# Two rounds of expert selection moved from the routing stage into the end of the first layer's attention

## The chip, the cores and the metric

The kernel runs on one core of a Trainium2 chip. Its engines work in parallel, each through its own instruction stream, and meet only at semaphores: TensorE (PE, with weight loads shown apart as PEld), VectorE (DVE), ScalarE (ACT), GpSimd (POOL) and SyncE (SP, which here only issues DMAs). The metric is the device time of one execution in microseconds, median of several; lower is better.

## The reference

Input x is 16 sequences of 256 tokens of 128 numbers, so 4096 tokens or 32 tiles of 128. Two layers follow, each x + s * g of the layer-normalised x.

- Layer 0: s is a gated linear recurrence (causal convolution, two sigmoid gates, scan, output matrix, RMS norm). g is the silu of a transformer block: layer norm, 16-head attention with heads of 8, output projection, residual, layer norm, then a mixture of 8 experts of which each token takes 2.
- Layer 1: s is attention with normalised queries and keys, g is a gated feed-forward net whose operands are rounded to blockwise FP4.

What the change touches is the choice of the two experts:

```
h = layernorm(x + attention)            # 4096 tokens x 128
logits = h @ gate_w + gate_b            # 4096 x 8
topv, topi = top_k(logits, 2)           # ties go to the lower expert
gw = softmax(topv)
ew = sum(one_hot(topi) * gw)            # weight of every expert for every token
moe = einsum(expert outputs, ew)
```

## The kernel before

The program is a row of phases: `phase_pre0` (norms, queries, keys, values), `phase_attention(0)`, `phase_moe`, `phase_update`, `phase_attention(1)`, `phase_ffn1`. Between two phases every engine meets at a barrier: each finishes its own instructions, POOL clears semaphores in between, and only then does any engine start on the next phase. Within a phase the order of each engine's work is written out by hand; there is no scheduler.

**Attention.** It goes sequence by sequence (b = 0 to 15), 16 steps each. PE computes scores and products, ACT the exponentials, and DVE takes the largest score of each query beforehand (`take_maximum`, L387, `neg_max`). The output of sequence b is divided, transposed and projected (`norm`, L1076 to L1087) during the next sequence, b+1. DVE then computes mean and variance (`statistics`, `variances`, ending in `ve`, L1107), and POOL's `rows_ready(c)` (L1017 to L1027) turns them into the normalised rows `hn` and the logits of the two tiles of sequence c, and increments `hn_ready`. SP stores `hn` to DRAM (L952) once `hn_ready` says so. The phase ends in a tail. In the last sequence DVE has no maxima left to take (they are always for the next sequence). After it come the three norm stages of sequence 15, its statistics, POOL's `rows_ready(15)`, and SP's last store, whose landing SP waits for before it goes to the barrier.

**Routing,** the start of `phase_moe`. DVE alone starts. It sets `one8` and `more_b` (the second is the multiplier of a scan that starts afresh at each expert), and then runs `best(0)` and `best(1)`: the largest logit of each token (`top`), which experts have it (`key`), times a falling order so that the lowest expert wins (`key`, `kmax`), and a one-hot mask (`mask`). Between the two the chosen logit is pushed far down. These are 11 instructions over 128 x 256 (32 tiles x 8 experts), each waiting for the one before (`link`). `sel` is the sum of both masks in another order, `upto` a running count; PE sums them over partitions, and DVE goes on to a place for every token, to slots, and to index lists. POOL's gathers and SP's weight loads wait for these lists. From there 72 slots of 128 tokens go through the experts.

The instructions of one step are waited for by a semaphore counter: `Steps.link` marks an instruction and waits for its mark before the next one.

Of the kernel before, what the change touches and what calls it, by code (L numbers as in the profile page):

```python
# [27 lines left out]
P = 128  # L28
# [8 lines left out]
E = 8  # L37
# [87 lines left out]
class Shared:  # L125
# [10 lines left out]
    def sem(self, name):  # L136
        return self.nc.alloc_semaphore(self.name(name))
# [18 lines left out]
def build(nc, x, vecs, b1v, mats, w1, w2, b2, gate_w, rows, gate_b, w4, consts, more, out):  # L156
    with ExitStack() as top:
# [55 lines left out]
        with ExitStack() as layer0:  # L213
# [14 lines left out]
            S.w2_sb = S.sb(experts, "w2", [P, E, FC, D])  # L228

# [587 lines left out]
def phase_attention(S, layer):  # L817
# [9 lines left out]
    with ExitStack() as ctx:  # L827
# [26 lines left out]
        if layer == 0:  # L854
# [5 lines left out]
            stats_done, mv_done, var_ready, rstd_ready, hn_ready, lg_scaled = (  # L860
                sem(n) for n in ("stats_done", "mv_done", "var_ready", "rstd_ready", "hn_ready", "lg_scaled"))
# [189 lines left out]
        def _(dve):  # L1051
# [79 lines left out]

            dve.sem_inc(bank_free, N_BANK)  # L1132
            if layer == 0:
                dve.sem_inc(hn_ready, 2)
            dve.memset(p_o[:], 0.0).then_inc(o_set, 1)
            sequences(dve, seq)
            for stage in range(len(NORM)):
                i = len(LAST) + stage
                consume(NB - 1, 1, base(NB - 1, "last") + i, bank_of("last", NB - 1, i), ("norm", stage))
            if layer == 0:  # L1140
                statistics(NB - 1, 1, base(NB - 1, "last") + len(LAST) + len(NORM) + N_BANK)
                variances(NB - 1, 1)

# [138 lines left out]
def phase_moe(S):  # L1282
# [4 lines left out]
    with ExitStack() as ctx:  # L1287
# [3 lines left out]
        key = sb("key", [P, N, E])  # L1291
        mask = [sb(f"mask{k}", [P, N, E]) for k in range(2)]
        top = [sb(f"top{k}", [P, N]) for k in range(2)]
        kmax = [sb(f"kmax{k}", [P, N]) for k in range(2)]
        gap, ex, den = sb("gap", [P, N]), sb("ex", [P, N]), sb("den", [P, N])
        sel, upto = sb("sel", [P, E, N], BF16), sb("upto", [P, E, N], BF16)
        more_b = sb("more_b", [P, E, N])
# [145 lines left out]
        def _(dve):  # L1443
            st = Steps(dve, steps)
            lg = S.logits

            def best(k):

                st.link(dve.tensor_reduce(top[k][:], lg[:], AX.X, ALU.max))
                st.link(dve.tensor_tensor(key[:], lg[:], of_tile(top[k]), ALU.is_equal))  # L1450
                st.link(dve.tensor_tensor(key[:], key[:], of_expert(const("order", E)), ALU.mult))
                st.link(dve.tensor_reduce(kmax[k][:], key[:], AX.X, ALU.max))
                st.link(dve.tensor_tensor(mask[k][:], key[:], of_tile(kmax[k]), ALU.is_equal))

            st.mark(dve.memset(one8[:], 1.0))
            st.link(dve.memset(more_b[:], 1.0))
            st.mark(dve.memset(more_b[:, :, 0:1], 0.0))
            best(0)
            st.link(dve.scalar_tensor_tensor(lg[:], mask[0][:], -3.0e38, lg[:], ALU.mult, ALU.add))
            best(1)  # L1460
# [1046 lines left out]
```

## Time and profile before

| | us |
|---|---|
| median of 3 runs | 1036.28 (1034.65 to 1038.63) |
| profiled execution, its own time | 1034.11 |
| its span, first to last instruction | 1032.3 |
| DVE busy | 806.2 (78%) |
| PE busy | 804.6 (78%) |
| ACT busy | 612.8 (59%) |
| POOL busy | 397.3 (38%) |
| mean granted TensorE clock | 0.881 of full speed |

The shares are averages over very different stages, and no engine is at its limit throughout. The stage that the change touches is short: the attention of layer 0 lies between about 80.9 and 293.9 us, and routing between 293.9 and about 325 us. What matters there is who waits for whom in those few microseconds, which the trace shows instruction by instruction. In its rows PEclk is the clock granted to TensorE, where 1.00 is 2.4 GHz and 0.50 is 1.2 GHz.

### The profile page before, as it was taken

What the parts mean: (1) busy time and instruction counts of PE and PEld (TensorE: products, weight loads), DVE (VectorE), ACT (ScalarE), POOL (GpSimd) and SP (SyncE); (2) the same over time, 40 slices, a digit from 0 to 9 for tenths busy, and PEclk for the clock granted to TensorE, in tenths of its full rate; (3) what the DMA queues carried; (4) which work ended last, traced back from release to release, by engine and by line L of the source; (5) the groups of instructions that cost most, each with busy time, mean ns of one, the idle gap of its engine ahead of it and who ended that gap; (6) DMA issues with size and microseconds to landing.
All of it is one profiled execution on the core that took longest, in us unless ns stands there. A gap on an engine that the chain in (4) does not pass through costs nothing. (4 is left out here: it accounts for less than half of the span.)

```text
span 1032.3 us, 23120 instructions
## 1 busy us (share of the span) xinstructions
PE 804.6 (78%) x6866; PEld 472.2 (46%) x6866; DVE 806.2 (78%) x1738; ACT 612.8 (59%) x1270; POOL 397.3 (38%) x684
## 2 busy tenths in 40 slices
PE   4888899999806788888896455649999999776764
PEld 3643333333305677776775233313333333345553
DVE  6758899999666345565663899889999998799984
ACT  3866677777705366566653478747777777433342
POOL 6852343333413666676673132231111211022332
PEclk9977999999955899999998666659999999888987
DMA  4692422222102343343342145532222221000001
GB/s 138 230 305 65 140 78 84 73 74 78 32 6 59 115 145 119 122 124 123 122 129 95 61 142 169 175 126 66 69 76 64 75 66 33 1 1 21 13 19 30
DMA packets 114716, 94.52 MB, mean 92 GB/s; under 512 B 10783, under 2 KB 102714, under 8 KB 114512
## 3 DMA queue, kind: packets, MB, share of 16 engines
q1 hardware_dynamic: 109104, 83.31, 25.9%
q0 software_dynamic: 4608, 8.93, 2.9%
q10 hardware_dynamic: 928, 1.32, 0.4%
q8 instruction: 41, 0.67, 0.3%
q14 instruction: 35, 0.29, 0.1%
HBM read 59.18 MB, written 34.08 MB: 90 GB/s over the span
## 5 line engine op out<-in xcount | busy, mean ns | idle before, releaser
L1157 ACT ACTIVATE pr<-score 128x512 f32<-128x512 f32 x512 | 279.1, 599 | 109.7 <-PE score L1225 109.6
L387 DVE TENSOR_REDUCE neg_max<-bank 128x2 f32<-128x512 f32 x480 | 303.7, 683 | 7.5 <-PE bank L371 6.3
L1225 PE MATMUL score<-qs,ks 51*128 51x256 bf16 x1024 | 179.3, 277 | 13.5 <-DVEq L1132 5.6
L371 PE MATMUL bank<-ks,qs 48*128 48x256 bf16 x960 | 168.4, 278 | 0.0
L1243 PE MATMUL p_o<-pr,vs 128*18 128x256 f32 x2048 | 164.2, 391 | 0.6 <-ACT pr L1157 0.6
L1225 PEld LDWEIGHTS score<-qs,ks 51*128 51x128 bf16 x1024 | 64.8, 95 | 155.7 <-DVE neg_max L387 49.3
L396 POOL TENSOR_TENSOR max_parts<-neg_max,one 128x16 bf16<-128x16 f32 x64 | 14.3, 223 | 268.6 <-DVE neg_max L387 259.9
L1428 POOL DMA_INDIRECT y_scratch<-y_all,to_i x72 | 79.9, 1109 | 56.0 <-DVE y_all L1529 45.1
L1644 ACT ACTIVATE hid<-p_ha,b_slot 128x128 f32<-128x128 f32 x144 | 44.9, 364 | 89.8 <-PE p_hd L1755 63.3
L1422 POOL DMA_INDIRECT y_all<-hn_scratch,token_i x72 | 76.1, 1056 | 55.6 <-DVEq L1510 34.0
L1529 DVE COPY y_all<-p_y 128x128 f32<-128x128 f32 x72 | 20.9, 290 | 83.3 <-PE p_y L1766 40.5
L1766 PE MATMUL p_y<-w,hid 128*128 x576 | 85.5, 293 | 0.0
L1766 PEld LDWEIGHTS p_y<-w,hid 128*128 128x128 f32 x576 | 71.5, 195 | 5.2
L1521 DVE TENSOR_SCALAR hid<-p_hd,b_slot 128x128 f32<-128x128 f32 x144 | 43.4, 343 | 24.8 <-PE p_hd L1755 19.6
L371 PEld LDWEIGHTS bank<-ks,qs 48*128 48x128 bf16 x960 | 60.5, 95 | 2.3
L285 POOL TENSOR_TENSOR hq<-hn,amax_h 128x1408 f32<-128x1408 f32 x7 | 18.1, 2589 | 102.6 <-DVE hn L263 102.6
L1243 PEld LDWEIGHTS p_o<-pr,vs 128*18 128x18 f32 x2048 | 36.2, 96 | 44.0 <-issue 30.8
L2413 PE MATMUL p_z<-wd_t,hq_t 128*128 128x128 f32 (+1 forms) x192 | 31.8, 340 | 22.4 <-ACT hq_t L2343 22.4
L1755 PE MATMUL p_ha<-h_t,w_now 128*128 128x128 f32 x288 | 46.2, 285 | 0.0
L1755 PE MATMUL p_hd<-h_t,w_now 128*128 128x128 f32 x288 | 46.0, 284 | 0.0
L2134 PE MATMUL p_qkv<-mat,xn_t 128*128 128x384 f32 x64 | 37.6, 757 | 7.4 <-ACT xn_t L2069 7.4
L2413 PEld LDWEIGHTS p_z<-wd_t,hq_t 128*128 128x128 f32 (+1 forms) x192 | 30.1, 249 | 24.7 <-ACT hq_t L2343 24.7
(324 smaller groups left out, 1645.0 us busy)
## 6 DMA issues: line engine op xcount, KB each, us to landing
w_now<-w_dram SPq DMA_DIRECT2D x72, 256.0 KB
ks<-k_scratch SPq DMA_DIRECT2D x128, 96.0 KB, 2.2
qs<-q_scratch SPq DMA_DIRECT2D x128, 96.0 KB, 2.3
k_scratch<-parts SPq DMA_DIRECT2D x16, 384.0 KB, 2.7
q_scratch<-parts SPq DMA_DIRECT2D x16, 384.0 KB, 3.0
k_scratch<-parts SPq DMA_DIRECT2D x16, 256.0 KB, 2.3
q_scratch<-parts SPq DMA_DIRECT2D x16, 256.0 KB, 2.6
both<-y_scratch SPq DMA_DIRECT2D x8, 512.0 KB, 4.0
```

The costliest lines, as they stand in the source:

```text
L371: return pe.matmul(bk[:, qt * L:(qt + 1) * L], S.qs[u][rows, place(h), qt * P:(qt + 1) * P], S.ks[u][rows, place(h), :], start=True, stop= ...
L387: return dve.tensor_reduce(S.neg_max[:, h // (H // 2), :, col:col + 1], bk[:].rearrange("p (q t) -> p q t", t=L), AX.X, ALU.max, negate=True)
L1157: act.activation(pr[s % N_PR][:, 2 * k:2 * k + 2, :], score[k][:], ACT.Exp, scale=SCALE).then_inc(exp_done, 1)
L1225: scored = pe.matmul(score[k][:, j, :], ks[u][rows, place(h), kt * P:(kt + 1) * P], qs[u][rows, place(h), :], start=True, stop=True)
L1243: last = pe.matmul(p_o[32 * j:32 * j + 2 * VW, hg // 2, 0:L], vs[u][:, kt, hg * JT + j, :], pr[s % N_PR][:, j, :], start=s % (STEPS // 2) ...
L1422: pool.indirect_dma_start(blk[j % U], None, S.hn_scr, bass.IndirectOffsetOnAxis(ap=token_i[:, j:j + 1], axis=0), bounds_check=last_token, ...
L1428: pool.indirect_dma_start(S.y_scr, bass.IndirectOffsetOnAxis(ap=to_i[:, j:j + 1], axis=0), y_out[j % U], None, bounds_check=last_row, oob_ ...
L1521: last = dve.tensor_scalar(hid[r][:, f, :], part(r, f), b1_slot[:, f, j:j + 1], 0.0, ALU.add, ALU.max)
L1644: last = act.activation(hid[r][:, f, :], part(r, f), ACT.Relu, bias=b1_slot[:, f, j:j + 1])
L1755: last = pe.matmul(part(r, f), w1_now[j % 3][:, f * P:(f + 1) * P], h2_t[r][:], start=True, stop=True)
L1766: last = pe.matmul(p_y[j % 2][:, 0:D], hid[j % 2][:, f, :], S.w2_sb[:, bass.ds(e, 1), f, :].rearrange("p o c -> p (o c)"), start=False, st ...
L2413: last = pe.matmul(p_z[:, n * D:(n + 1) * D], hq_t[0:w, i, n * P:(n + 1) * P], S.wd_t[0:w, i, :], start=i == 0, stop=i == len(K_CHUNKS) - 1)
```

## The change

A new function `best_two(first, end)` holds both rounds, for the tiles first to end. DVE runs it twice inside `phase_attention(0)`: over tiles 0 to 27 right after the last sequence's own work and before the norm stages of sequence 15, and over tiles 28 to 31 after the variances of sequence 15. Each call first waits for POOL's `hn_ready`: for the logits of sequence 13, or of sequence 15. The masks, `top` and `more_b` are allocated in the scope that spans both phases. The two memsets of `more_b`, with a wait between them, go to the start of DVE's attention work, in front of the memset of `p_o`. The routing stage begins with `sel`, and `one8` is set behind the scan.

```diff
--- before.py
+++ after.py
@@ -226,6 +226,9 @@
             S.both = [S.sb(layer0, f"both{u}", [P, NT, 2, D]) for u in range(2)]
             experts = layer0.enter_context(ExitStack())
             S.w2_sb = S.sb(experts, "w2", [P, E, FC, D])
+            S.mask = [S.sb(experts, f"mask{k}", [P, S.NTILE, E]) for k in range(2)]
+            S.top = [S.sb(experts, f"top{k}", [P, S.NTILE]) for k in range(2)]
+            S.more_b = S.sb(experts, "more_b", [P, E, S.NTILE])
 
 
             with nc.cleanup_on_exit():
@@ -857,8 +860,10 @@
                              for n, shape in (("mv", [2, 2]), ("ve", [2]), ("x_now", [2, ROW])))
             hn = [sb(f"hn{u}", [P, 2, D]) for u in range(2)]
             lg_raw = sb("lg_raw", [P, 2, E])
-            stats_done, mv_done, var_ready, rstd_ready, hn_ready, lg_scaled = (
-                sem(n) for n in ("stats_done", "mv_done", "var_ready", "rstd_ready", "hn_ready", "lg_scaled"))
+            key, kmax = sb("key", [P, S.NTILE, E]), [sb(f"kmax{k}", [P, S.NTILE]) for k in range(2)]
+            stats_done, mv_done, var_ready, rstd_ready, hn_ready, lg_scaled, steps_top, more_set = (
+                sem(n) for n in ("stats_done", "mv_done", "var_ready", "rstd_ready", "hn_ready", "lg_scaled", "steps_top",
+                                 "more_set"))
             hn_kept = [sem("hn_kept0"), sem("hn_kept1")]
         else:
             NX = GROUP // BLK
@@ -1129,17 +1134,41 @@
                     if layer == 1 and kind == "last" and s == 4:
                         first_input()
 
+            def best_two(first, end):
+
+                dve.wait_ge(hn_ready, end // 2 + 2)
+                now = slice(first, end)
+                shape = [P, end - first, E]
+                lg, keys = S.logits[:, now, :], key[:, now, :]
+                order = S.more[:, MORE["order"]:MORE["order"] + E].unsqueeze(1).broadcast_to(shape)
+                of_tile = lambda t: t[:, now].unsqueeze(2).broadcast_to(shape)
+                for k in range(2):
+                    if k:
+                        to.link(dve.scalar_tensor_tensor(lg, S.mask[0][:, now, :], -3.0e38, lg, ALU.mult, ALU.add))
+                    to.link(dve.tensor_reduce(S.top[k][:, now], lg, AX.X, ALU.max))
+                    to.link(dve.tensor_tensor(keys, lg, of_tile(S.top[k]), ALU.is_equal))
+                    to.link(dve.tensor_tensor(keys, keys, order, ALU.mult))
+                    to.link(dve.tensor_reduce(kmax[k][:, now], keys, AX.X, ALU.max))
+                    to.link(dve.tensor_tensor(S.mask[k][:, now, :], keys, of_tile(kmax[k]), ALU.is_equal))
+
             dve.sem_inc(bank_free, N_BANK)
             if layer == 0:
+                to = Steps(dve, steps_top)
                 dve.sem_inc(hn_ready, 2)
+                dve.memset(S.more_b[:], 1.0).then_inc(more_set, 1)
+                dve.wait_ge(more_set, 1)
+                dve.memset(S.more_b[:, :, 0:1], 0.0)
             dve.memset(p_o[:], 0.0).then_inc(o_set, 1)
             sequences(dve, seq)
+            if layer == 0:
+                best_two(0, 2 * (NB - 2))
             for stage in range(len(NORM)):
                 i = len(LAST) + stage
                 consume(NB - 1, 1, base(NB - 1, "last") + i, bank_of("last", NB - 1, i), ("norm", stage))
             if layer == 0:
                 statistics(NB - 1, 1, base(NB - 1, "last") + len(LAST) + len(NORM) + N_BANK)
                 variances(NB - 1, 1)
+                best_two(2 * (NB - 2), 2 * NB)
 
         @block.scalar
         def _(act):
@@ -1288,13 +1317,9 @@
         sb = lambda n, shape, dt=F32: S.sb(ctx, n, shape, dt)
         sem = S.sem
 
-        key = sb("key", [P, N, E])
-        mask = [sb(f"mask{k}", [P, N, E]) for k in range(2)]
-        top = [sb(f"top{k}", [P, N]) for k in range(2)]
-        kmax = [sb(f"kmax{k}", [P, N]) for k in range(2)]
+        mask, top, more_b = S.mask, S.top, S.more_b
         gap, ex, den = sb("gap", [P, N]), sb("ex", [P, N]), sb("den", [P, N])
         sel, upto = sb("sel", [P, E, N], BF16), sb("upto", [P, E, N], BF16)
-        more_b = sb("more_b", [P, E, N])
         above = sb("above", [P, N, E])
         nb, ends, start, one8 = sb("nb", [P, E]), sb("ends", [P, E]), sb("start", [P, E]), sb("one8", [P, E])
         place, picked = sb("place", [P, N, E]), [sb(f"picked{k}", [P, N, E]) for k in range(2)]
@@ -1442,26 +1467,11 @@
         @block.vector
         def _(dve):
             st = Steps(dve, steps)
-            lg = S.logits
-
-            def best(k):
-
-                st.link(dve.tensor_reduce(top[k][:], lg[:], AX.X, ALU.max))
-                st.link(dve.tensor_tensor(key[:], lg[:], of_tile(top[k]), ALU.is_equal))
-                st.link(dve.tensor_tensor(key[:], key[:], of_expert(const("order", E)), ALU.mult))
-                st.link(dve.tensor_reduce(kmax[k][:], key[:], AX.X, ALU.max))
-                st.link(dve.tensor_tensor(mask[k][:], key[:], of_tile(kmax[k]), ALU.is_equal))
-
-            st.mark(dve.memset(one8[:], 1.0))
-            st.link(dve.memset(more_b[:], 1.0))
-            st.mark(dve.memset(more_b[:, :, 0:1], 0.0))
-            best(0)
-            st.link(dve.scalar_tensor_tensor(lg[:], mask[0][:], -3.0e38, lg[:], ALU.mult, ALU.add))
-            best(1)
             by_expert = lambda t: t[:].rearrange("p n e -> p e n")
             st.link(dve.tensor_tensor(sel[:], by_expert(mask[0]), by_expert(mask[1]), ALU.add))
             flat = lambda t: t[:].rearrange("p e n -> p (e n)")
             dve.tensor_tensor_scan(flat(upto), flat(more_b), flat(sel), 0.0, ALU.mult, ALU.add).then_inc(sel_ready, 1)
+            st.mark(dve.memset(one8[:], 1.0))
             dve.tensor_tensor(gap[:], top[1][:], top[0][:], ALU.subtract).then_inc(gap_ready, 1)
 
             dve.wait_ge(counted, 1)
```

On DVE, around the end of the attention and the start of routing, this stood in a row before (the two branches are the phase boundary; `o_rec` to `ve_193` are the norm stages and statistics of sequence 15):

```order
L1107 TENSOR_SCALAR ve_192<-mv_190 128x2
L1076 RECIPROCAL o_rec<-bank_168 128x32
...
L1107 TENSOR_SCALAR ve_193<-mv_191 128x2
L827 UNCONDITIONAL_BRANCH
L1442 UNCONDITIONAL_BRANCH
L1455 MEMSET one_224 128x8
L1456 MEMSET more_b 128x256
L1457 MEMSET more_b 128x8
L1449 TENSOR_REDUCE top_210<-logits 128x32
L1450 TENSOR_TENSOR key<-logits,top_210 128x256
...
L1453 TENSOR_TENSOR mask_209<-key,kmax_213 128x256
L1462 TENSOR_TENSOR sel<-mask_208,mask_209 128x256
```

The same place of the changed kernel:

```order
L1112 TENSOR_SCALAR ve_197<-mv_195 128x2
L1148 TENSOR_REDUCE top_84<-logits 128x28
L1149 TENSOR_TENSOR key<-logits,top_84 128x224
...
L1152 TENSOR_TENSOR mask_83<-key,kmax_206 128x224
L1081 RECIPROCAL o_rec<-bank_173 128x32
...
L1112 TENSOR_SCALAR ve_198<-mv_196 128x2
L1148 TENSOR_REDUCE top_84<-logits 128x4
L1149 TENSOR_TENSOR key<-logits,top_84 128x32
...
L1152 TENSOR_TENSOR mask_83<-key,kmax_206 128x32
L830 UNCONDITIONAL_BRANCH
L1467 UNCONDITIONAL_BRANCH
L1471 TENSOR_TENSOR sel<-mask_82,mask_83 128x256
```

The 11 selection instructions over 256 columns are now 11 over 224 ahead of `o_rec`, and 11 over 32 between `ve` and the boundary.

On DVE at the start of the attention, before:

```order
L461 UNCONDITIONAL_BRANCH
L1050 UNCONDITIONAL_BRANCH
L1135 MEMSET p_o 128x1024
L387 TENSOR_REDUCE neg_max<-bank_168 128x2
```

and in the changed kernel:

```order
L464 UNCONDITIONAL_BRANCH
L1055 UNCONDITIONAL_BRANCH
L1158 MEMSET more_b 128x256
L1160 MEMSET more_b 128x8
L1161 MEMSET p_o 128x1024
L390 TENSOR_REDUCE neg_max<-bank_173 128x2
```

Two memsets now stand ahead of `p_o` and of the first maximum. On PE, ACT, POOL and SP no instruction moves.

## Rows read from the trace of the kernel before

**Rows 1.** Who waited for whom, 274 to 325 us: total, times, longest.

```profile
DVE one L1455 <- PEq L233: 6.1, 1, 6.1
PE p_y L1724 <- DVE upto L1464: 14.6, 1, 14.6
```

**Rows 2.** Stretches: length; busy (count) PE, PEld, DVE, ACT, POOL; PEclk; DMA; GB/s.

```profile
80.90:87.80 6.90, 6.45 (x54) 2.29 (x58) 5.44 (x9) 3.81 (x8) 2.77 (x9) 0.50 0.01 4
...
278.60:283.30 4.70, 3.72 (x36) 1.19 (x36) 0.02 (x1) 3.08 (x7) 3.00 (x6) 1.00 0.10 31
...
293.90:299.30 5.40, 0.00 (x0) 0.00 (x0) 4.96 (x14) 0.00 (x0) 0.00 (x0) 0.50 0.01 2
...
345.00:350.00 5.00, 5.00 (x20) 3.69 (x18) 1.10 (x4) 0.98 (x3) 2.42 (x3) 0.50 0.22 81
355.00:360.00 5.00, 4.37 (x36) 3.82 (x35) 2.31 (x7) 3.80 (x10) 3.11 (x3) 1.00 0.45 153
```

**Rows 3.** DVE in time, routing: start, us, line, operation, [idle before <- releaser].

```profile
293.89 0.07 DVE L1455 MEMSET one<- 128x8 f32 x1 [6.08 <-PEq L233]
293.97 0.27 DVE L1456 MEMSET more_b<- 128x256 f32 x1
294.29 0.41 DVE L1449 TENSOR_REDUCE top<-logits 128x32 f32<-128x256 f32 x1
...
299.31 0.62 DVE L1462 TENSOR_TENSOR sel<-mask,mask 128x256 bf16<-128x256 f32 x1
...
301.38 0.42 DVE L1468 TENSOR_TENSOR above<-p_y,more 128x256 f32<-128x256 f32 x1 [0.65 <-PE p_r L1726]
```

**Rows 4.** DVE in time, end of the last sequence.

```profile
278.45 0.17 DVE L1107 TENSOR_SCALAR ve<-mv 128x2 f32<-128x2 f32 x1
283.39 0.36 DVE L1076 RECIPROCAL o_rec<-bank 128x32 f32<-128x32 f32 x1 [4.77 <-PE bank L1193]
```

**Rows 5.** POOL in time, rows and logits of sequences 13, 14 and 15.

```profile
274.67 0.22 POOL L1027 TENSOR_TENSOR logits<-lg_raw,gshift 128x16 f32<-128x16 f32 x1
278.77 0.72 POOL L1017 TENSOR_TENSOR rstd<-ve,m_half 128x2 f32<-128x2 f32 x1 [3.88 <-DVE ve L1107]
...
281.55 0.22 POOL L1027 TENSOR_TENSOR logits<-lg_raw,gshift 128x16 f32<-128x16 f32 x1
...
290.73 0.22 POOL L1027 TENSOR_TENSOR logits<-lg_raw,gshift 128x16 f32<-128x16 f32 x1
```

**Rows 6.** SP's last store of hn in time, and landing times of all of them.

```profile
290.97 0.37 SPq L952 DMA_DIRECT2D hn_scratch<-hn  x1
...
DMA to landing us min/median/max: 1.8/1.9/4.9
```

**Rows 7.** DVE in time, linked short instructions in routing.

```profile
302.69 0.17 DVE L1472 TENSOR_TENSOR start<-ends,nb 128x8 f32<-128x8 f32 x1
302.89 0.42 DVE L1473 SCALAR_TENSOR_TENSOR place<-start,p_r 128x256 f32<-128x256 f32 x1
...
305.73 0.23 DVE L1482 TENSOR_TENSOR hi<-at,lo 128x64 f32<-128x64 f32 x1
305.99 1.36 DVE L1486 TENSOR_TENSOR by_slot<-more,hi 128x1152 bf16<-128x1152 f32 x1
```

**Rows 8.** DVE and POOL in time, last phase: one DVE instruction twice.

```profile
1001.61 1.63 DVE L263 SCALAR_TENSOR_TENSOR hn<-hn,hm 128x1408 f32<-128x1408 f32 x1
...
1014.32 2.57 DVE L263 SCALAR_TENSOR_TENSOR hn<-hn,hm 128x1408 f32<-128x1408 f32 x1
...
1014.06 1.35 POOL L2218 TENSOR_TENSOR o<-z,s_all 128x512 f32<-128x512 f32 x1 [5.58 <-ACT z L2349]
```

**Rows 9.** DVE in time, start of the attention, and what it waited for, 81 to 92 us.

```profile
80.89 0.91 DVE L1135 MEMSET p_o<- 128x1024 f32 x1 [1.99 <-PEq L231]
81.71 0.68 DVE L387 TENSOR_REDUCE neg_max<-bank 128x2 f32<-128x512 f32 x1
...
DVE neg_max L387 <- PE bank L371: 1.5, 3, 0.7
```

## The prediction

> **What bounds the kernel now.** I read the busy shares first and then left them, since they average over unlike stages. The stage that the change touches is told by the list of who waited for whom: from 274 to 325 us the first DVE instruction of routing waited 6.1 us for the phase boundary, and PE waited 14.6 us for `upto`, an instruction of DVE's routing chain [rows 1]. The table of stretches agrees: from 293.90 to 299.30 PE, ACT and POOL do nothing at all, and DVE works through 14 instructions, 4.96 of 5.40 us [rows 2]. So DVE alone is the path there, and what leaves this stretch leaves the total, unless it comes back on a path elsewhere. Then I read the instructions in time: routing [rows 3], the gap in DVE's last sequence [rows 4], what POOL does in it [rows 5], and who comes last to the boundary [rows 6]. Everything behind routing (gathers, weight loads, 72 slots) starts from its lists and shifts with it.
>
> **What is removed.** From 293.89, where `one8` is set, to 299.31, where `sel` starts: 5.42 us [rows 3]. The 11 linked instructions are 294.29 to 299.31, 5.02 us or 0.456 us each. `one8` goes into DVE's wait for PE ahead of 301.38 (0.65 us) and costs nothing. The phase boundary ahead of `sel` is kept. Term: -5.42.
>
> **The head of the attention.** Two memsets stand ahead of `p_o`. In routing the first, with its wait, took 293.97 to 294.29 and `one8`, as long as the second, took 0.08, so 0.32 + 0.08 = 0.40 us [rows 3]. `p_o` and the first maximum follow without a gap in DVE (80.89 and 81.71, [rows 9]), and DVE's queue then holds all later maxima, on which PE's row products and SP's stores of maxima hang. Against that, DVE waits for PE's products 1.5 us in the next microseconds [rows 9], since TensorE is at 1.2 GHz from 80.90 to 87.80 (0.50, [rows 2]). So part of the delay is swallowed. Bounds 0.1 and 0.4; I take 0.30, near the upper end, since PE soon waits for the same chain. Term: +0.30.
>
> **The first part, 28 tiles.** It starts behind `ve` (278.45). Its logits are there: those of sequence 13 were done at 274.67 + 0.22 = 274.89 [rows 5]. Per instruction I interpolate: 0.456 us over 256 columns, 0.26 us over 64 (305.73 to 305.99, [rows 7]), so 1.02 ns a column, and 0.424 us over 224. Eleven are 4.66 us. Starting at about 278.57 they end at 283.23, and `o_rec` started at 283.39, when PE was done [rows 4]. The work fits into the hole with 0.16 us to spare, if nothing slows it.
>
> Something may. DVE was empty in the hole (0.02 us busy, [rows 2]) but POOL was not: it ran `rows_ready(14)` from 278.77 to 281.77 [rows 5]. In the last phase the same DVE instruction with two SBUF operands took 1.63 us alone and 2.57 us when a POOL instruction had started 0.26 us ahead of it and still had 1.09 us to run [rows 8]: DVE lost 0.94, nearly all of POOL's rest. Seven of the eleven instructions read two SBUF tensors (the four others are reductions with one). The first POOL instruction, a power over 2 columns, reads next to nothing; the rest, about 279.44 to 281.77, is 2.3 us. If every bit of it stops DVE once, DVE is late by 2.3 - 0.16, so 2.1 us; if none does, by 0. Put in order by hand, with each engine waiting for the other's piece and the reductions running beside POOL, DVE loses about 1.2 and is late by 1.0. That is also the middle, and I take it. `o_rec` stands at the head of a chain of DVE and PE up to `ve` and `rows_ready(15)`, so its delay counts in full. Term: +1.0.
>
> The Trainium skill (SBUF — State Buffer, "SBUF: two separate sides") has a rule for this: DVE and GpSimd share one pair of ports under an exclusive lock that is held for a whole instruction, and a DVE instruction with two SBUF inputs needs it against a GpSimd one that reads SBUF. The trace agrees in the pair just named, 2.57 against 1.63. By the rule without exception the term is near its upper end; without the rule it is 0.
>
> **The second part, 4 tiles, and the boundary.** Logits 15 are done at 290.95; SP's last store, released by the same semaphore, starts at 290.97, so DVE can start then too. It lands about 1.9 us later, at 292.85, and DVE's next phase begins at 293.89 [rows 3, 6]: 1.04 us from the last arrival to the first instruction. Eleven instructions over 32 columns: the nearest rows are 0.20 us from start to start over 8 columns and 0.26 over 64 [rows 7], so 0.225 each, 2.48 in all. DVE is done at 293.45, 0.6 us after the store. So DVE takes SP's place as the last at the boundary. By the two rows the eleven take 2.20 to 2.86, which makes 0.3 to 1.0; I take 0.6. Term: +0.60. Queued behind these instructions is only DVE's branch to the boundary, but all five engines wait there.
>
> The page "VectorE: DVE Perf Modes" of the Trainium skill ("The TRN2 errata") gives (N + 151)/0.96 ns for such an instruction and warns that many small tiles pay the fixed part each time. It gives 191 ns for 32 columns, which no row has, and 424 ns for 256; the row has 0.42. That speaks against splitting 11 instructions into 22: the fixed part is paid twice.
>
> **Sum.** -5.42 + 0.30 + 1.0 + 0.6 = -3.5 us. The profiled execution took 1034.11 us (span 1032.3, and 1.8 around it), so its like would take 1030.6. The median of the runs is 2.2 above that execution, so I put the sum on the median: 1036.28 - 3.5 = 1032.8. The runs before lie from 1034.65 to 1038.63, about 2 us either way.
>
> **Rivals.**
> 1. *No blocking.* POOL's pieces are short and DVE's reads slip in between. Then the first part is free, and the sum is -5.42 + 0.3 + 0.6 = -4.5, or -5.0 with both other terms at their lower ends (0.1 and 0.3). Time 1031.3 to 1031.8. For it: POOL's instructions here move 16 to 256 columns, those of [rows 8] 512. Against: POOL still needs 2.3 us for them.
> 2. *Full blocking and a late boundary.* -5.42 + 0.4 + 2.1 + 1.0 = -1.9, so 1034.4. Against: the reductions run beside POOL.
> 3. *Slower than before: TensorE's clock in the expert stage.* This stage is PE's: from 345 to 350 us PE was busy 5.00 of 5.00 and did 20 matmuls at a granted 0.50, from 355 to 360 it did 36 at 1.00 [rows 2]. So 5 us at 1.2 GHz do the work of 2.8 at 2.4 GHz, and lose 2.2. The stage starts about 4 us earlier, and its pauses, in which the clock fell, stand elsewhere against the moments at which the chip changes the clock. To lose 3.5 us takes 8 us more at the lower clock; with two more stretches of 5 us the change is slower: -3.5 + 4.4 = +0.9, or 1037.2. Against: DVE's and PE's order in that stage is unchanged and pauses come with the loads, so it must be chance. In the other direction, one stretch less gives -5.7 and 1030.6.
> 4. *It doesn't do what it says:* part one would find its logits late and stop DVE. The row of sequence 13 is 3.6 us early [rows 4, 5], so I give it nothing.
>
> **How the numbers follow.** The forecast, -3.5, has 0.55 and its own range is 1031.0 to 1034.5 (first part 0.3 to 1.8, boundary 0.3 to 0.9). Rival 1 has 0.22, rival 2 has 0.11, rival 3 upwards 0.06 and downwards 0.06. About 0.5%, 5.2 us, is what a measurement can tell from no change; faster by more means under 1031.1. That is nearly all of the downward clock case (0.05), something under half of rival 1 (0.09) and a little of the forecast's lower end (0.04): 0.18. Slower by more means over 1041.5 and needs 20 us more at the lower clock: 0.02. The rest, 0.80, is within 0.5%. The range takes in rivals 1 and 2 with the scatter of a median: 1029.8 to 1036.0.
>
> **What would show it.** (a) `sel` starts about 1.0 us after the last engine reaches the boundary and nothing of DVE stands ahead of it. (b) Part one: if its two-tensor instructions take more than 0.39 us while POOL runs, the lock is at work; the start of `o_rec` against PE's last transpose gives the term. If `o_rec` still waits for PE, the term is 0. (c) Part two: 11 instructions of about 0.19 us, and DVE's last mask ends after the store of hn lands. (d) The first `neg_max` of the attention starts 0.4 us later after the boundary. The forecast is wrong if logits 15 to `sel`, 8.36 us before (290.95 to 299.31), is not 3.5 to 3.6 us, or if attention as a whole grows by more than 2 us.

## The result and the profile after

| | before | after |
|---|---|---|
| median of this comparison, us | 1036.16 (1033.78 to 1038.63, 6 runs) | 1028.72 (1028.13 to 1030.23, 6 runs) |
| ratio | | 0.9923 [0.9904, 0.9942] |
| profiled execution, us (span) | 1034.11 (1032.3) | 1029.58 (1027.8) |
| predicted | | 1032.8 (1029.8 to 1036.0) |

The change makes the kernel faster, by 7.4 us between the medians and by 4.5 us between the two profiled executions. Forecast were 3.5 us, and the median of 1028.7 lies 1.1 us below the range. So the two questions are which term was too pessimistic, and whether the 7.4 us belong to the kernel.

The page of the changed kernel, its head and the clock in 40 slices. It says little, since 5 us are half a percent of the span: DVE's busy time has not changed (806.2 before), it only stands elsewhere.

```profile
span 1027.8 us, 23133 instructions
## 1 busy us (share of the span) xinstructions
PE 808.2 (79%) x6866; PEld 476.2 (46%) x6866; DVE 805.8 (78%) x1749; ACT 611.6 (60%) x1270; POOL 395.0 (38%) x684
...
PEclk9978999999955899999997666659999999788885
```

Who waited for whom in the changed kernel, 272 to 320 us (total, times, longest), answers to [rows 1]:

```profile
PEld p_y L1734 <- DVE upto L1473: 10.0, 1, 10.0
PE p_y L1734 <- DVE upto L1473: 9.8, 1, 9.8
...
DVE top L1148 <- POOL logits L1032: 3.2, 1, 3.2
...
DVE sel L1471 <- PEq L236: 1.1, 1, 1.1
```

PE's wait for `upto` went from 14.6 to 9.8 us, and that is the gain: 4.8. DVE's 6.1 us of waiting for the boundary have become 3.2 for POOL's last logits and 1.1 for the boundary; in the rest it works.

DVE in the changed kernel from the end of the last sequence (start, us, line, operation, [idle before <- releaser]) answers to [rows 3, 4]:

```profile
276.95 0.17 DVE L1112 TENSOR_SCALAR ve<-mv 128x2 f32<-128x2 f32 x1
277.03 0.38 DVE L1148 TENSOR_REDUCE top<-logits 128x28 f32<-128x224 f32 x1
277.44 0.39 DVE L1149 TENSOR_TENSOR key<-logits,top 128x224 f32<-128x224 f32 x1
...
279.14 0.44 DVE L1147 SCALAR_TENSOR_TENSOR logits<-mask,logits 128x224 f32<-128x224 f32 x1
...
280.46 0.44 DVE L1150 TENSOR_TENSOR key<-key,more 128x224 f32<-128x224 f32 x1
...
281.35 0.39 DVE L1152 TENSOR_TENSOR mask<-key,kmax 128x224 f32<-128x224 f32 x1
281.97 0.36 DVE L1081 RECIPROCAL o_rec<-bank 128x32 f32<-128x32 f32 x1 [0.23 <-PE bank L1222]
...
286.14 0.17 DVE L1112 TENSOR_SCALAR ve<-mv 128x2 f32<-128x2 f32 x1
289.47 0.19 DVE L1148 TENSOR_REDUCE top<-logits 128x4 f32<-128x32 f32 x1 [3.17 <-POOL logits L1032]
...
291.71 0.19 DVE L1152 TENSOR_TENSOR mask<-key,kmax 128x32 f32<-128x32 f32 x1
292.99 0.62 DVE L1471 TENSOR_TENSOR sel<-mask,mask 128x256 bf16<-128x256 f32 x1 [1.09 <-PEq L236]
...
295.06 0.42 DVE L1478 TENSOR_TENSOR above<-p_y,more 128x256 f32<-128x256 f32 x1 [0.62 <-PE p_r L1736]
```

Three things are to be seen. The first part fills the hole and `o_rec` still waits 0.23 us for PE, so DVE is not late. The second part starts with POOL's logits and ends at 291.90; `sel` follows after 1.09 us of boundary. And `one8` has vanished into the wait ahead of `above` (0.62; 0.65 before, [rows 3]).

POOL beside the first part, of the changed kernel. In [rows 5] the same `logits` instruction starts 2.78 us after `rstd` (281.55 - 278.77), here 3.18:

```profile
277.26 0.72 POOL L1022 TENSOR_TENSOR rstd<-ve,m_half 128x2 f32<-128x2 f32 x1 [3.90 <-DVE ve L1112]
277.94 0.57 POOL L1024 COPY rows<-x_now 128x256 f32<-128x256 f32 x1
278.47 0.21 POOL L1026 TENSOR_TENSOR lg_raw<-x_now,rstd 128x16 f32<-128x16 f32 x1
278.67 1.79 POOL L1029 TENSOR_SCALAR hn<-x_now,mv,rstd 128x128 f32<-128x128 f32 x2
280.44 0.21 POOL L1032 TENSOR_TENSOR logits<-lg_raw,gshift 128x16 f32<-128x16 f32 x1
...
287.13 0.40 POOL L1024 COPY rows<-x_now 128x256 f32<-128x256 f32 x1
```

The two engines do get in each other's way, but the loser is POOL: its copy takes 0.57 us beside DVE and 0.40 alone ten microseconds later, its pair of `hn` 1.79 us beside DVE and 1.57 alone. Nobody waits for POOL here.

The stretches that answer to [rows 2] (length; busy (count) PE, PEld, DVE, ACT, POOL; PEclk; DMA; GB/s): the start of the attention, the hole, the old place of the work.

```profile
79.50:86.50 7.00, 6.42 (x54) 2.28 (x58) 5.58 (x11) 3.78 (x8) 2.84 (x10) 0.50 0.01 4
277.20:281.90 4.70, 3.68 (x36) 1.16 (x34) 4.20 (x11) 2.97 (x7) 3.39 (x6) 1.00 0.07 22
286.20:293.00 6.80, 0.00 (x0) 0.00 (x0) 2.20 (x13) 0.00 (x0) 2.99 (x6) 0.50 0.06 19
```

And DVE at the start of the attention, answering to [rows 9]; the first `neg_max` starts 1.57 us after the boundary's release, 1.12 before:

```profile
79.49 0.27 DVE L1158 MEMSET more_b<- 128x256 f32 x1 [2.11 <-PEq L234]
79.83 0.07 DVE L1160 MEMSET more_b<- 128x8 f32 x1
80.11 0.91 DVE L1161 MEMSET p_o<- 128x1024 f32 x1 [0.21 <-issue]
80.93 1.22 DVE L390 TENSOR_REDUCE neg_max<-bank 128x2 f32<-128x512 f32 x2
```

Milestones of several profiled executions, as distances in us. "Release" is POOL's first instruction of the attention; "y first to last" is the distance between DVE's first and last copy of a slot's output (`y_all`):

| kernel | release to first maximum | to `ve` of 14 | to `o_rec` of 15 | to `ve` of 15 | to end of logits 15 | to `sel` | y first to last | last y to end |
|---|---|---|---|---|---|---|---|---|
| before | 1.12 | 196.74 | 4.94 | 4.24 | 3.31 | 8.37 | 217.8 | 475.4 |
| after | 1.57 | 196.02 | 5.02 | 4.17 | 3.30 | 3.55 | 213.3 | 478.1 |
| before_again | 1.12 | 198.22 | 4.94 | 4.17 | 3.30 | 8.38 | 192.2 | 478.5 |
| after_again | 1.57 | 197.63 | 5.02 | 4.18 | 3.30 | 3.55 | 192.3 | 476.4 |

In these four the columns up to `sel` repeat to 0.1 us, except the long one (first maximum to `ve` of 14), which differs by up to 2 us between profiles of the same code. In five later profiles, of kernels with and without the change, `o_rec` to `ve` of 15 takes 4.6 to 4.7 us. The last two columns differ by several us.

That the first pair of profiles lies 4.5 us apart, close to the 4.8 of routing, is luck: the release comes 1.2 us earlier in the changed one, the way from `sel` to the first y is 3.5 us longer (43.4 and 39.9), from the first y to the last it is 4.5 us shorter, and the rest is 2.8 us longer.

### The profile page after: what moved, and what is told of

It reads as the page before. It is cut to its first block and busy times, and to the rows that moved or that the text cites. A ratio compares the mean times of both kernels' runs of the same rounds, so it can differ in the third digit from the quotient of the medians.

```text
span 1027.8 us, 23133 instructions
## 1 busy us (share of the span) xinstructions
PE 808.2 (79%) x6866; PEld 476.2 (46%) x6866; DVE 805.8 (78%) x1749; ACT 611.6 (60%) x1270; POOL 395.0 (38%) x684
## 5 line engine op out<-in xcount | busy, mean ns | idle before, releaser
L1447 POOL DMA_INDIRECT y_all<-hn_scratch,token_i x72 | 74.6, 1036 | 50.8 <-DVEq L1520 29.1
L1531 DVE TENSOR_SCALAR hid<-p_hd,b_slot 128x128 f32<-128x128 f32 x144 | 43.4, 342 | 26.7 <-PE p_hd L1765 17.9
L2423 PE MATMUL p_z<-wd_t,hq_t 128*128 128x128 f32 (+1 forms) x192 | 38.7, 390 | 23.5 <-ACT hq_t L2353 23.5
L2423 PEld LDWEIGHTS p_z<-wd_t,hq_t 128*128 128x128 f32 (+1 forms) x192 | 36.9, 298 | 25.8 <-ACT hq_t L2353 25.8
```

Source lines behind the costliest of these rows:

```text
L1447: pool.indirect_dma_start(blk[j % U], None, S.hn_scr, bass.IndirectOffsetOnAxis(ap=token_i[:, j:j + 1], axis=0), bounds_check=last_token, ...
L1531: last = dve.tensor_scalar(hid[r][:, f, :], part(r, f), b1_slot[:, f, j:j + 1], 0.0, ALU.add, ALU.max)
L2423: last = pe.matmul(p_z[:, n * D:(n + 1) * D], hq_t[0:w, i, n * P:(n + 1) * P], S.wd_t[0:w, i, :], start=i == 0, stop=i == len(K_CHUNKS) - 1)
```

## The experiments

Two theories stood at the start. **A**: all of the gain is the shorter path of routing, -4.8 us, nothing of it is given back, and the rest of the -7.4 us is scatter. **B**: there is a second source, the new addresses of the masks (B1) or something behind routing that profits from the earlier start.

**Both kernels again, on another chip.** No edit.

> The kernel before itself, timed against itself, to see how far two sets of its runs lie apart and how its profile differs from the first one. Every theory expects a ratio of 1.000 within its interval. If stages that nobody touched (the prologue, the expert stage, the last phase) differ by 1 to 3 us between two profiles, the -1.2 us of the prologue and the up and down behind routing in the profile of the changed kernel are scatter.

> The changed kernel once more. Theory A (the gain is the path that left routing, and what the median showed beyond it is scatter of few runs): 4.3 to 4.9 us under the kernel before. Theory B (some 3 us more are real and come from another effect): 7 to 8 us under it, as in the first comparison.

Measured: the kernel before 1008.32 us under its second name, 1007.87 under its first (ratio 1.0007 [0.9987, 1.0028]); the changed one 1003.11, ratio 0.9949 [0.9927, 0.9970]. All times are about 28 us shorter on this chip, nearly all of it in the expert stage (192 us between the first and the last y, 218 before). The saving is 4.8 us here. Routing is the same to 0.01 us.

**The addresses alone.** The kernel before, with the masks, `top` and `more_b` where the changed kernel has them (`key` and `kmax` go to the end of the expert stage's tiles, where neither kernel has them):

```diff
             S.w2_sb = S.sb(experts, "w2", [P, E, FC, D])
+            S.mask = [S.sb(experts, f"mask{k}", [P, S.NTILE, E]) for k in range(2)]
+            S.top = [S.sb(experts, f"top{k}", [P, S.NTILE]) for k in range(2)]
+            S.more_b = S.sb(experts, "more_b", [P, E, S.NTILE])
...
-        mask = [sb(f"mask{k}", [P, N, E]) for k in range(2)]
+        mask, top, more_b = S.mask, S.top, S.more_b
```

> Of the change, only where the tiles lie in SBUF: the masks, the maxima and more_b are allocated beside the expert weights as in the changed kernel, and key and kmax at the end of the expert stage's tiles; every instruction stays where it was before. Theory B1 (the unexplained 3 us come from other addresses of the tiles in the attention or the expert stage): 2.5 to 3.5 us faster than before. Rival A: no change, within 1 us.

Measured: 1007.75, ratio 0.9998 [0.9979, 1.0016]. That leaves no room for the 2.5 to 3.5 us of B1, on a chip with the short expert stage; on one with the long stage it was not tried.

**The saving put back.** The changed kernel with the 14 old instructions at the start of routing, on scratch tiles that nothing reads:

```diff
             st = Steps(dve, steps)
+            st.mark(dve.memset(one2[:], 1.0))
+            st.link(dve.memset(more2[:], 1.0))
+            st.mark(dve.memset(more2[:, :, 0:1], 0.0))
+            for k in range(2):
...
```

> The changed kernel with the 14 old instructions put back at the start of routing, on scratch tiles that nothing reads, so that routing takes as long as before while everything else is as in the changed kernel. Theory A (the path of routing is all): 0.3 to 1.3 us slower than before, by the head (0.3 to 0.4), the first part (0.1) and the boundary (0.6). Theory B1 (addresses): still 2 to 3 us faster than before. Theory B2 (the later stages gain by starting earlier, through the clock or the loads): like theory A, since they start as late as before again.

Measured: 1008.43, ratio 1.0009 [0.9990, 1.0027]; logits 15 to `sel` 9.00 us, 0.63 more than before. That is the boundary term by itself: with all old work in routing, the second part only makes DVE the last at the boundary. DVE's row there, of this kernel: the last mask of part two ends at 291.99 and `one2` waits 1.12 us.

```profile
291.80 0.19 DVE L1152 TENSOR_TENSOR mask<-key,kmax 128x32 f32<-128x32 f32 x1
293.11 0.07 DVE L1472 MEMSET one<- 128x8 f32 x1 [1.12 <-PEq L236]
...
298.53 0.62 DVE L1484 TENSOR_TENSOR sel<-mask,mask 128x256 bf16<-128x256 f32 x1
```

**No split.** All 32 tiles in the second place, none in the first:

```diff
-                best_two(0, 2 * (NB - 2))
...
-                best_two(2 * (NB - 2), 2 * NB)
+                best_two(0, 2 * NB)
```

> The changed kernel with one call for all 32 tiles in the second place (behind the variances of sequence 15) and none in the first. Theory (11 linked instructions cost 0.456 us each over 256 columns, and the tail is path from the last logits on): logits of sequence 15 to sel grows from 3.55 to 11 x 0.456 + 1.1 = 6.1 us, the chain from ve of sequence 14 to o_rec goes back by 0.1, and the kernel stands 2.4 us behind the changed one, about 2.3 us ahead of the one before. Rival (what counted was only to leave routing, since the store of hn hides the tail): 3.6 us between logits and sel, as in the changed kernel.

Measured: 1005.36, ratio 0.9979 [0.9962, 0.9997], logits 15 to `sel` 6.12 us. DVE in that kernel, in steps of 0.457 us:

```profile
292.48 0.42 DVE L1148 TENSOR_REDUCE top<-logits 128x32 f32<-128x256 f32 x1 [3.17 <-POOL logits L1032]
292.94 0.43 DVE L1149 TENSOR_TENSOR key<-logits,top 128x256 f32<-128x256 f32 x1
```

Nearly half of the saving, 2.25 us (8.37 - 6.12), needs no hole at all: about 0.4 are the memsets taken out of routing, and the rest is the stretch between the logits and the release of the boundary, in which DVE idled before. The split brings the other 2.6 us (6.12 - 3.55), and the fixed part of eleven more short instructions is no objection, since the 28-tile ones lie in the hole.

**The memsets in a wait.** They go from the head of the attention to DVE's wait for POOL's last rows:

```diff
-                dve.memset(S.more_b[:], 1.0).then_inc(more_set, 1)
-                dve.wait_ge(more_set, 1)
-                dve.memset(S.more_b[:, :, 0:1], 0.0)
...
                 variances(NB - 1, 1)
+                dve.memset(S.more_b[:], 1.0).then_inc(more_set, 1)
+                dve.wait_ge(more_set, 1)
+                dve.memset(S.more_b[:, :, 0:1], 0.0)
```

> The changed kernel with the two memsets of more_b in DVE's wait for POOL ahead of the second part. Theory (head term 0.3 to 0.4): from the boundary to the first neg_max 0.40 us less than in the changed kernel, the attention of layer 0 up to ve of sequence 14 shorter by 0.1 to 0.4, nothing added in the tail (DVE waits 3.2 us there). Rival (DVE's waits for PE swallow the head): the first neg_max earlier, ve of sequence 14 at the same distance from the boundary. In the total 0 to 0.4 us, under what a comparison of runs can tell.

Measured: 1003.90, ratio 0.9962 [0.9946, 0.9979]. In the trace the local cost is gone, 1.12 us to the first maximum as before, and the second part starts no later. In the time nothing of it can be seen: the changed kernel on the same chip had 1002.60 (after_third). The 0.45 us at the head are too few to be told in the time. The traces show no sign that they are passed on: from the release to `ve` of 14 the eight profiles with the memsets at the head, extra POOL work left out, take 197.5 to 199.2 us (mean 198.3) and the seven without 197.9 to 200.1 (mean 199.0).

**Logits first.** On top of that edit, POOL computes the logits ahead of `hn` and signals them by themselves:

```diff
-                for n in range(2):
-                    pool.tensor_scalar(hn[u][:, n, :], ...)
...
-                                   ).then_inc(hn_ready, 1)
+                                   ).then_inc(lg_ready, 1)
+                for n in range(2):
+                    last = pool.tensor_scalar(hn[u][:, n, :], ...)
+                last.then_inc(hn_ready, 1)
...
-                dve.wait_ge(hn_ready, end // 2 + 2)
+                dve.wait_ge(lg_ready, end // 2)
```

> Like the one with the memsets in the wait, and POOL computes the logits ahead of hn, with a semaphore of their own for DVE. Theory (DVE's second part is the last at the boundary, 0.66 us behind the store): DVE starts its second part 1.6 us earlier, ends ahead of the store's landing, and the last ve to sel shrinks by 0.5 to 0.7 us, since the store is last again; 0.9 to 1.1 us under the changed kernel in all. Rival (the shared port stops DVE beside hn): part two grows by up to 1.5 us and the gain is gone.

> The changed kernel on the same chip as these three, for comparison. Theory A: 4.3 to 4.9 us under the kernel before, as the second set of runs had it (4.8); theory B (7 to 8 us, as in the first comparison).

Measured: 1003.02, ratio 0.9949 [0.9929, 0.9969], beside 1002.60, ratio 0.9947 [0.9927, 0.9968], of the unedited changed kernel. From `ve` of 15 to `sel` it is 6.33 us instead of 6.85, as expected, but the total doesn't show the half microsecond, nor the 0.9 to 1.1 us that were expected with the head. DVE of logits_early:

```profile
289.44 0.18 DVE L1150 TENSOR_REDUCE top<-logits 128x4 f32<-128x32 f32 x1 [1.32 <-POOL logits L1030]
...
290.35 0.30 DVE L1154 TENSOR_TENSOR mask<-key,kmax 128x32 f32<-128x32 f32 x1
...
291.80 0.19 DVE L1154 TENSOR_TENSOR mask<-key,kmax 128x32 f32<-128x32 f32 x1
293.87 0.62 DVE L1473 TENSOR_TENSOR sel<-mask,mask 128x256 bf16<-128x256 f32 x1 [1.88 <-PEq L236]
```

and its store, of SP:

```profile
290.99 0.37 SPq L958 DMA_DIRECT2D hn_scratch<-hn  x1
```

DVE is done at 291.99 and waits 1.88 us. This store lands 1.8 us after its issue at 290.99, at 292.8, and `sel` follows 1.1 us later: SP is the last at the boundary again, as it was before [rows 6]. So here the second part is free, and the store is the floor.

**What POOL costs DVE.** The disputed term by itself: the changed kernel with extra POOL work beside the first part, four adds over 512 columns (pool_wide) or six `tensor_scalar` over 128 (pool_narrow), ahead of `rows_ready(14)`. Both also set the scratch tile with one memset at the head of POOL's attention. Of pool_wide:

```diff
+                if layer == 0 and c == NB - 2:
+                    pool.wait_ge(var_ready, NB - 1)
+                    for i in range(4):
+                        pool.tensor_tensor(idle_b[:, i, :], idle_a[:], idle_a[:], ALU.add)
```

> The changed kernel with four more POOL instructions, each an addition over 512 columns from SBUF to SBUF on scratch tiles, beside DVE's first part (they wait for the same variances as rows_ready(14), which comes after them). Theory L1 (a POOL instruction holds the shared port for all of its recorded time): DVE's two-tensor instructions beside them take up to 1.3 us instead of 0.39, and the first part grows by 3 to 5 us. Theory L2 (it holds it for its columns' traffic only): 512 columns of two operands are long enough to hold it nearly throughout, so nearly the same, 2 to 4 us.

> The same with six POOL instructions like those of hn (a subtraction and a product with a scalar for each partition, 128 columns) in place of the four, about as long in all (6 x 0.79 = 4.7 us). Theory L1: the first part grows as much as beside the wide ones. Theory L2 (what stops DVE is the columns' traffic, 128 columns or about 0.1 us, and most of the recorded 0.79 us is the instruction's own overhead): under 0.5 us, some two-tensor instructions 0.05 to 0.1 us longer.

DVE and POOL in pool_wide:

```profile
277.95 0.38 DVE L1156 TENSOR_REDUCE top<-logits 128x28 f32<-128x224 f32 x1
278.36 1.04 DVE L1157 TENSOR_TENSOR key<-logits,top 128x224 f32<-128x224 f32 x1
279.44 1.11 DVE L1158 TENSOR_TENSOR key<-key,more 128x224 f32<-128x224 f32 x1
280.59 0.39 DVE L1159 TENSOR_REDUCE kmax<-key 128x28 f32<-128x224 f32 x1
281.01 0.69 DVE L1160 TENSOR_TENSOR mask<-key,kmax 128x224 f32<-128x224 f32 x1
281.74 1.11 DVE L1155 SCALAR_TENSOR_TENSOR logits<-mask,logits 128x224 f32<-128x224 f32 x1
...
278.12 4.48 POOL L1060 TENSOR_TENSOR idle_b<-idle_a 128x512 f32<-128x512 f32 x4 [3.82 <-DVE ve L1120]
```

and in pool_narrow:

```profile
277.24 0.47 DVE L1157 TENSOR_TENSOR key<-logits,top 128x224 f32<-128x224 f32 x1
277.75 0.39 DVE L1158 TENSOR_TENSOR key<-key,more 128x224 f32<-128x224 f32 x1
...
279.02 0.53 DVE L1155 SCALAR_TENSOR_TENSOR logits<-mask,logits 128x224 f32<-128x224 f32 x1
...
281.77 0.36 DVE L1089 RECIPROCAL o_rec<-bank 128x32 f32<-128x32 f32 x1
...
277.03 5.32 POOL L1060 TENSOR_SCALAR idle_b<-idle_a,one,eps_c 128x128 f32<-128x128 f32 x6 [3.85 <-DVE ve L1120]
```

Measured: one execution each, 1004.13 and 1001.68 us, beside 1007.03 of the kernel before. With the wide instructions DVE's two-tensor operations take up to 1.11 us instead of 0.39, 2.4 us more in the four that are shown, and the reductions still 0.39; `ve` to `o_rec` grows from 5.02 to 7.20 us. With the narrow ones POOL is busy for 5.32 us, over the whole first part (six at 0.79 us alone would be 4.7), and DVE loses 0.23 us (0.08 + 0.14 + 0.01); `ve` to `o_rec` stays 5.02. So POOL's recorded time is no measure of what DVE loses: 4.48 us of it cost 2.4, 5.32 us cost 0.23. Theory L1 asked for 3 to 5 us in both and got 2.2 and 0 on the path; what L2 asked for, 2 to 4 and under 0.5, fits both. Whether it is the width, the second operand or the operation that makes the wide ones dear isn't told apart.

**Where the -7.4 us come from.** A chip with the long expert stage (from the first to the last y) was met once more:

> The kernel before under a second name, as a measure of how far two equal kernels lie apart. Every theory: a ratio of 1.000 with an interval of about 0.002 either way. If it comes out 0.3% or more from 1, an excess of 2.7 us in the first comparison needs no cause in the kernel.

> The changed kernel once more, beside its own kernel before. Theory A, the saving is what the routing path shows (-4.82) with +0.1 for the first part and 0 to +0.45 for the head: -4.3 to -4.7 us, a ratio of 0.9953 to 0.9958, whatever the chip; the rest of the -7.4 of the first comparison is scatter. Theory B, where the expert stage is long (about 231 us from the first slot's index to the last slot's output, as on the first chip, against 203 on the second) the changed kernel gains some 3 us more: the ratio is 0.992 if this chip's stage is the long one, and 0.995 if it is the short one. The stage's length in this trace tells which prediction of B applies; with 203 us both say 0.995 and nothing is told apart.

Measured: the second name of the kernel before 1043.15, its first 1041.23 (ratio 1.0016 [0.9987, 1.0045]); the changed one 1034.88, ratio 0.9940 [0.9916, 0.9964]. The stage was long (225.5 and 218.3 us from the first to the last y), and the interval holds the answers of both theories. The two names of the same code came out 0.16% apart, less than the 0.3% that would have explained the excess by itself. So a last set:

> The changed kernel. Theory A (scatter): 0.9953 to 0.9958 on any chip. Theory B (extra gain where the expert stage is long, y0 to y71 over 213 us instead of 192): 0.992 to 0.993 if the stage is long here, 0.995 if it is short.

> The kernel before with the masks, the tops and the scan's multiplier allocated where the changed kernel has them; nothing moves in time. If the extra gain of B comes from the addresses: 0.997 to 0.998 where the stage is long. Otherwise 1.000, as it was with the short stage (0.9998).

> The changed kernel with the 14 old instructions put back at the start of routing on scratch tiles, so that the expert stage starts about 0.6 us later than before. Theory A: 1.0005 to 1.001. Theory B with a cause that is not the saved routing time: 0.997 to 0.998 where the stage is long. Theory B with the earlier start as its cause: 1.0005 to 1.001 too.

Measured, with the short stage (192 us): 0.9931 [0.9910, 0.9953], 1.0001 [0.9985, 1.0018] and 1.0005 [0.9988, 1.0022]. The ratio is below 0.994 though the stage is short, so the one comparison that looked like more gain with a long stage has a counterpart with a short one. Theory B's 0.995 for a short stage lies inside the interval too, so this alone excludes nothing, and the expectation of A, 0.9953 to 0.9958, is at the interval's edge.

The five comparisons of the changed kernel (0.9923, 0.9949, 0.9947, 0.9940, 0.9931), weighted by the inverse squares of their half-widths, give 0.9937 [0.9928, 0.9947]. The unchanged code under other names or addresses gives 1.0003 [0.9993, 1.0013] over its four, the refilled kernel 1.0007 [0.9994, 1.0019] over its two. On 1008 us the gain is 6.3 us (5.3 to 7.3). The first of the five is the one that raised the question. The four that were made to answer it give 0.9942 [0.9931, 0.9953], 5.8 us (4.8 to 6.9). By stage, the three with the short one give 0.9942 and the two with the long one 0.9930, 0.0013 apart with 0.0019 either way.

## Why the prediction was wrong, point by point

**What bounds the kernel, and what is removed (-5.42): right.** PE's wait for `upto` shrank by 4.8 us, which is 5.42 less the boundary term. `one8` is hidden. With the 14 instructions back the gain is gone (1.0009, 1.0005).

**Second part and boundary (+0.60): right.** Logits 15 to `sel` took 3.55 us, within the forecast's 3.5 to 3.6. The eleven instructions take 0.18 to 0.19 us and start 0.225 apart, as interpolated. routing_refilled measures the term alone, +0.63. The formula on the page "VectorE: DVE Perf Modes" of the Trainium skill ("The TRN2 errata"), (N + 151)/0.96 ns, makes an estimate of 191 ns for 32 columns, and the trace agrees: 0.19.

**Head (+0.30): locally 0.45, of the total nothing that can be told.** The first maximum comes 0.45 us later behind the boundary, and 0 later in memsets_in_wait. Whether the attention passes it on was not settled: its length scatters by 2 us, and the profiles with the memsets at the head are not the longer ones (198.3 against 199.0 us in the mean).

**First part (+1.0): this is the step that failed.** "DVE loses about 1.2 and is late by 1.0" took the pair in [rows 8], where a DVE instruction lost nearly all that remained of a POOL instruction over 512 columns, and applied it to POOL instructions over 16 to 256 columns by their recorded time. The measured loss is two times 0.05 us in the eleven instructions, and `o_rec`, which still waits for PE, starts 0.08 us later behind `ve` (5.02 instead of 4.94; unsplit_tail, without the first part, has 4.94 again). PE's last transpose starts 4.63 us behind `ve` with and without the first part, so the 0.08 are not PE's; what they are is not shown. The price per microsecond of POOL was taken from the wrong kind of instruction: four of 512 columns put 2.2 us on the path (pool_wide), six of the kind that stands here put nothing on it (pool_narrow). The rule of the Trainium skill (SBUF — State Buffer, "SBUF: two separate sides") is borne out in which DVE instructions it names, those with two SBUF inputs and not the reductions. As a price, held for a whole instruction, it is not: 5.32 us of POOL cost DVE 0.23. Rival 1, a first part that is free, was right in its sum; it had been named with the argument that holds so far (the pieces are narrow), and too small a chance. Its time, 1031.3 to 1031.8, is not the measured one either.

**The sum and the reference.** With what the traces show, -4.82 + 0.08 + a head of 0 to 0.45, it is -4.7 to -4.3 us, close to rival 1. That alone would have made 1031.5 to 1032.0 of the median of 1036.28, inside the range. So of the 4.1 us between the forecast and the measured median the first part explains 0.9 and the head at most 0.3, and the first comparison came out about 3 us under what the terms give. No term of the prediction stands for these 3 us. All later comparisons lie between -4.8 and -6.4 us, so a part of the -7.4 may well be scatter, for which the range had no room: it was built from the sum's bounds, and gave the median of a few runs hardly anything, though single runs before lay 4 us apart. The 0.80 that it gave to a change within 0.5% missed for the same reason: the first comparison shows 0.77%, all together 0.63%.

**What stays open.** The mean of all comparisons, -5.3 to -7.3 us, is 0.6 to 3.0 more than the terms; that of the four later ones, -4.8 to -6.9, all but touches them. The changed kernel with the memsets moved, and with the logits first as well, carries the whole gain too, and came out at 0.9962 and 0.9949, no better than the terms. So an excess may be there, but it is not shown. Of its possible causes, the addresses were tried on the short stage alone (0.9998 and 1.0001), and the length of the expert stage is neither borne out nor excluded. The excess goes with the shortened routing as far as can be told, since the refilled kernel lies at 1.0007 and the terms ask for 1.0007 to 1.0012, but its interval leaves 1.3 us either way. The distance from the refilled kernel, 0.9937 to 1.0007, is 7.0 us with about 1.6 either way, and the profiles put `sel` 5.45 us apart (9.00 - 3.55), at the lower edge of that. In the profiles up to the last y the saving is 5.0 us (528 to 523 us, three of either kind with the short stage); behind it the unchanged code takes 476 to 478.6 us in either kernel. If there is more, it lies there or in the intervals' own error, and no run here tells which.

Rival 3, TensorE's clock in the expert stage, is answered by the traces. From the first to the last y (length; busy (count) PE, PEld, DVE, ACT, POOL; PEclk; DMA; GB/s), of before, after, before_again and after_again:

```profile
339.20:556.90 217.70, 188.96 (x1339) 158.01 (x1340) 119.14 (x339) 125.47 (x343) 143.36 (x133) 0.97 0.39 123
336.40:549.60 213.20, 188.57 (x1339) 157.62 (x1340) 118.78 (x339) 125.04 (x343) 139.89 (x130) 0.96 0.40 124
334.80:527.00 192.20, 182.95 (x1366) 154.59 (x1365) 119.13 (x339) 123.97 (x343) 144.38 (x135) 1.00 0.45 141
330.40:522.60 192.20, 182.87 (x1365) 154.50 (x1364) 119.11 (x339) 123.98 (x343) 144.41 (x135) 1.00 0.45 141
```

With the short stage the granted clock is 1.00 in both kernels and the stage is equally long, so there the clock gives nothing either way. In the first pair the changed kernel had no higher clock (0.96 and 0.97) and PE was as long busy; its stage is shorter by waits of PE. Behind the stage the clock changes between 0.50 and 1.00 at other moments in every profile, and what that does can't be told.

**Signs.** (a) `sel` comes 1.09 us after the last engine: right. (b) Two two-tensor instructions take 0.44 instead of 0.39, so POOL does reach DVE, but `o_rec` waits for PE, so the term is nearly 0. (c) and (d) right. Neither of the two signs of being wrong came: logits 15 to `sel` took 3.55 us, and the attention did not grow by 2 us. They watched the terms, and the miss in the median lies mostly outside them.

## What to carry to other kernels

Work of a stage in which one engine runs alone is worth moving into a hole of that engine even when it is cut in two for it, and what a moved piece costs is read at the next instruction of the chain: if that still waits for another engine, the piece is free. Before a contention seen on one pair of instructions is charged to another, compare their widths and kinds, not their times. And a range for a change of half a percent needs room for the comparison itself: here a comparison of identical code has an interval of 2 us of 1008 either way, and of 3 us of 1041 on the chip with the widest scatter. Two single profiles can agree with a sum by luck; compare them stage by stage.

## What the runs showed of the hardware

- POOL and DVE: four 512-column adds on POOL stretch two-tensor instructions of DVE over 224 columns from 0.39 to as much as 1.11 us; six 128-column `tensor_scalar` stretch three of seven, to 0.53 at most. POOL pays as well: a 256-column copy takes 0.57 us beside DVE and 0.40 alone.
- The boundary of attention and routing costs 1.09 to 1.12 us from DVE's last instruction to its first of the next phase where DVE is the last to come, and about 1.1 from the landing of the last store where the store is (before, logits_early).
- The same kernel takes 1008 us on some chips and 1036 to 1041 on others. The difference is mostly in the expert stage, by the rows of before and before_again under "What stays open": from the first y to the last PE is busy 182.95 of 192.2 us at a granted clock of 1.00 on one chip, and 188.96 of 217.7 us at 0.97 on the other, while weights and rows come in at 141 and 123 GB/s. So 6 of the 25.5 us are longer PE work and 19.5 are PE's waits. What makes PE wait longer was not tried.
